# Second layer of a two-layer FFN kernel: x1's rows turned and gathered, output written by rows, stores issued by ScalarE

## Chip, cores and metric

The kernel runs on one core of one Trainium2 chip. The metric is the device time in microseconds (us) of one execution.

## The reference, cut to what matters

`x` has 32 samples of 128 channels by 2048 positions. Layer 0 ends in `x1`; the change is in layer 1 alone, and in how its inputs and outputs are moved.

```python
x = x + L0_ffn(L0_cond(x))                              # x1, the first layer
# layer 1, cond: nine taps, four groups of 32 channels, a bias of each sample and channel
z = conv_general_dilated(x1, weight, padding=[(4, 4)], feature_group_count=4)
z = z + ctx[:, :, None] + bias[None, :, None]
# layer 1, ffn: every row (sample, channel) of 2048 is permuted, cut into 16 heads of 128
t = z.reshape(b * l, Dm)[:, perm].reshape(b * l, h, d)
t = gelu(einsum('bhd,hdm->bhm', t, up), approximate=False)      # 128 -> 512
t = einsum('bhm,hmd->bhd', t, down).reshape(b * l, h * d)       # 512 -> 128
out = x1 + t[:, unperm]
```

## The kernel before, in words

Layer 1 works in 128 **units** and 128 **steps**. A unit `u` is the convolution of one sample and one group of 32 channels: four row blocks of 32 channels are loaded side by side into 128 partitions (`load_group`, L88, four loads), split by ScalarE (`xp_hi`, L1467) and VectorE (`xp_lo`, L1537) into a high and a low part, and multiplied on TensorE in nine products of 512 columns (L1426) into `ps_c`. ScalarE adds the bias and writes `z_s` (L1496), VectorE turns it in squares of 32 (L1559) into a tile in SBUF that has room for four units, and after each fourth unit (`u % 4 == 3`) the tile is stored to the DRAM scratch `z_d` by four stores, one for each 32 partitions (L1305, issued by SyncE). In `z_d` a row is a position, so that a permuted gather by rows does the `perm`.

A **block** is 16 units (four tiles) and then 16 steps, one for each head; there are 8 blocks. In step `s` GpSimd gathers 128 permuted rows of `z_d` into `t_s` (L1352, three steps ahead); ScalarE and VectorE split them (`t_hi` L1473, `t_lo` L1543); TensorE makes four `up` parts of three products (L1401) into `ps_up`; ScalarE takes the gelu of each into `kern` (L1479); the result is split into `g_hi` (a cast: parts 0 and 2 by ScalarE, L1483, parts 1 and 3 by VectorE, L1579) and `g_lo` (VectorE, L1581); TensorE makes four `down` parts of three products (L1411) into `ps_y`. ScalarE copies `ps_y` to `y_room` (L1516), and GpSimd scatters it to the rows of a second scratch, `y_d` (L1383), which does the `unperm`.

One block later SyncE loads rows of `y_d` back (L1269, pairs of steps), VectorE turns them (L1564) and adds x1 (L1570), which SyncE has loaded into `rear` (L1275), and SyncE stores the output (L1293). For the last block this would come at the end: there `y_d` is loaded into `w_hi`, TensorE transposes it (L1452), VectorE adds x1 (L1613) and SyncE and ScalarE store `out` (L1172).

All engines run the same sequence of steps, each with its own part: `LEAD` = 20, so step `s` has the convolution of unit `u = s + 20` beside it, and 20 units come ahead of step 0 (the **lead**). In a step TensorE makes the nine products of the convolution, then the parts `down(s, mc)` and `up(s+1, mc)` in turn. Each engine does its work in the order in which the program names it, its DMA issues too; a wait (`wait_ge`) for a semaphore holds all that stands behind it on that engine.

```python
            def store_z(k, h, parity):
                sp.wait_ge(zt_ready, u + 1)
                for r in range(2 if isinstance(u, int) and u == H - 1 else S):
                    sp.dma_start(z_rows(z_d[(parity + ahead) % 2], r, jb),
                                 zt_of(k, h)[r * GC:(r + 1) * GC].rearrange("p w b c -> p w (b c)")).then_inc(z_out[jb % 2], 16)
```

Of the kernel before, what the change touches and what calls it, by code (L numbers as in the profile page):

```python
# [28 lines left out]
Y_LO = 576  # L29
# [29 lines left out]
class Shared:  # L59
# [25 lines left out]
    def load_group(self, eng, x1_d, xp, j, b, g):  # L85

        for s in range(S):
            eng.dma_start(xp[s * GC:(s + 1) * GC, 1:Q + 1],  # L88
                          x1_d[b, g * GC:(g + 1) * GC, s, :]).then_inc(self.xp_in[j], 16)

# [55 lines left out]
def layer0_block(nc, block, sh, x, cond_w, bias_k, cond_t, w0, b0, w1, b1, w2, b2, w_t, bias, lora_a, lora_b, coeffs, scales,  # L146
                 conv_w, ctx_w, fside, ident, up, down, aggb_d, aggw_d, weff_d, t_d, u_d, x1_d):

    with ExitStack() as ctx:
# [43 lines left out]
        with ExitStack() as next_up:  # L193
            sh.ps_up = next_up.enter_context(nc.psum_tensor("ps_up", [P, MC, 512], F32))
# [860 lines left out]
def layer1_block(nc, block, sh, x1_d, up, down, perm, ident, z_d, y_d, out):  # L1055

    with ExitStack() as ctx:
# [16 lines left out]
        t_hi, t_lo = ([sb(f"{n}{j}", [P, RB], F32R) for j in range(2)] for n in ("t_hi", "t_lo"))  # L1074
        g_hi, g_lo = sb("g_hi", [P, MC, RB], F32R), sb("g_lo", [P, MC, RB], F32R)
        rear = sb("rear", [P, 4, 4 * P])
        yt_s, x1_s = (rear[:, 2 * j:2 * j + 2, :].rearrange("p a n -> p (a n)") for j in range(2))
        results = sb("results", [P, 2, 512])
        o_s = results[:].rearrange("p a n -> p (a n)")
        with ExitStack() as ahead:  # L1080
            second = ahead.enter_context(nc.sbuf_tensor("second_xp", [P, Y_LO + Q + 2], F32R))
        y_room = sb("y_room", [P, Y_LO + Q + 4])
        y_s = [y_room[:, j * Y_LO:j * Y_LO + RB] for j in range(2)]
        idx = sb("idx", [P, H], I32)
        id_s = sb("id_s", [P, P])
        xp, t_s, cbias = sh.xp + [o_s[:, 0:Q + 2]], sh.t_s, sh.cbias
        g_s = sh.kern[:].rearrange("p (c n) -> p c n", c=MC)

        zt_pair = [flat.rearrange("p (w b c) -> p w b c", w=WIDE, b=SB)
                   for flat in (sh.x1_s[:].rearrange("p a n -> p (a n)"), rear[:].rearrange("p w n -> p (w n)"))]  # L1090

        ps_up = sh.ps_up
        bank("up_room", MC)
        ps_c, ps_last = bank("ps_c"), bank("ps_last")
        ps_y = [bank(f"ps_y{j}") for j in range(2)]

        small_in, w_in = sem("small_in"), sh.w_in
# [3 lines left out]
        z_ready, zt_ready = sem("z_ready"), sem("zt_ready")  # L1101
        z_out = [sem(f"z_out{j}") for j in range(2)]
        t_in = [sem(f"t_in{j}") for j in range(2)]
# [59 lines left out]
        def last_unit(v):  # L1163

            return v % 4, v // 4
# [520 lines left out]
```

## Time and profile before

| | |
|---|---|
| median of 3 runs | 2507.52 us (2507.34 to 2511.15) |
| the profiled execution | 2513.49 us, its span 2511.7 us, mean clock of TensorE 0.989 |
| busy share of the span | TensorE 97%, VectorE 68%, ScalarE 44%, GpSimd 37% |
| first layer | up to about 1450 us |
| lead of the second layer | about 1460 to 1528 us |
| steps with a convolution | up to about 2346 us |
| steps without | up to 2479 us, then the last block's output up to 2512 us |

The profile is of one execution. Busy times are sums over an engine's instructions; the granted clock is a share of 2.4 GHz, so that 0.50 is 1.2 GHz. T is used for the moment at which a step's convolution begins. "SPq" and "ACTq" are the times for which the sequencers of SyncE and ScalarE are at DMA issues.

### The profile page before, as it was taken

The numbers are of one execution on the slowest core, as the hardware profiler recorded it, in microseconds if no ns is written. First come the engines' busy times: TensorE is split into PE (matmuls) and PEld (weight loads), VectorE is DVE, ScalarE is ACT, GpSimd is POOL, SyncE is SP. The second block draws the span as 40 slices with busy tenths as digits, with TensorE's granted clock in tenths as the row PEclk, the third lists the DMA queues.
The fourth block names the chain that finished last, engine by engine and source line by source line (L and its number), as shares of the span: only waits on it lengthen the run. The fifth ranks groups of instructions, "written<-read, shape, count | busy, mean of one in ns | idle before, by whom it ended". The sixth has DMA issues, their size and how long they took to land.

```text
span 2511.7 us, 37065 instructions
## 1 busy us (share of the span) xinstructions
PE 2432.4 (97%) x11130; PEld 2010.9 (80%) x11130; DVE 1713.9 (68%) x2449; ACT 1113.7 (44%) x1850; POOL 938.1 (37%) x826
## 2 busy tenths in 40 slices
PE   8899999999999999999999988999999999999985
PEld 6788888888888888887888866888888888888864
DVE  6665555875555855558544665778888888888865
ACT  3221211321212322223222356777777777777753
POOL 2275654556645255323233311222222222222331
PEclk9999999999999999999999999999999999999988
DMA  8965554755543767657555665468888888888898
GB/s 301 326 214 187 199 174 159 258 177 205 202 163 132 269 219 225 204 178 258 178 172 172 194 196 153 141 189 244 242 245 248 240 240 243 245 246 245 231 245 255
DMA packets 397563, 540.90 MB, mean 215 GB/s; under 512 B 37016, under 2 KB 262640, under 8 KB 397360
## 3 DMA queue, kind: packets, MB, share of 16 engines
q1 hardware_dynamic: 295872, 309.50, 43.0%
q10 hardware_dynamic: 77376, 152.17, 16.2%
q0 software_dynamic: 24112, 76.80, 9.9%
q8 instruction: 93, 1.52, 0.2%
q14 instruction: 110, 0.90, 0.1%
HBM read 309.72 MB, written 228.61 MB: 214 GB/s over the span
## 4 chain that ended last, share of the span: by engine, by line
PE 88%; DMA 5%; DVE 3%; issue 2%; SPq 1%; ACT 1%; POOL 0%; ACTq 0%; DVEq 0%; POOLq 0%
PE ps_c L463 45%; PE ps_up L1401 13%; PE ps_y L1411 13%; PE ps_c L1426 9%; PE ps_v L441 4%; PE ps_c L429 3%; DMA u_s<-z_d,idx 1%; DVE w_lo L1006 1%; PE ps_up L1426 1%; SPq L88 1%; DMA rear<-x_d 1%; DVE ring_lo L953 1%; DMA w_hi<-y_d 1%; DMA x_n<-in_up 0%; DVE x_s L1002 0%
## 5 line engine op out<-in xcount | busy, mean ns | idle before, releaser
L463 PE MATMUL ps_c<-w_hi,ring_hi 128*128 128x512 f32 x1792 | 703.9, 393 | 4.9 <-DVE r_early L1002 3.6
L463 PE MATMUL ps_c<-w_hi,ring_lo 128*128 128x512 f32 x1792 | 698.0, 390 | 0.0
L463 PE MATMUL ps_c<-w_lo,ring_hi 128*128 128x512 f32 x1792 | 697.9, 389 | 0.0
L613 ACT ACTIVATE ring_hi<-raw_n 128x512 fp32r<-128x512 f32 x382 | 239.6, 631 | 852.2 <-DVE raw_n L944 232.1
L1581 DVE TENSOR_TENSOR g_lo<-kern,g_hi 128x512 fp32r<-128x512 f32 x512 | 349.2, 687 | 80.3 <-ACT g_hi L1483 71.3
L463 PEld LDWEIGHTS ps_c<-w_hi,ring_hi 128*128 128x128 f32 x1792 | 336.8, 188 | 75.8 <-DVE ring_lo L953 4.7
L463 PEld LDWEIGHTS ps_c<-w_hi,ring_lo 128*128 128x128 f32 x1792 | 336.5, 188 | 69.8
L463 PEld LDWEIGHTS ps_c<-w_lo,ring_hi 128*128 128x128 f32 x1792 | 336.8, 188 | 67.5
L1383 POOL DMA_INDIRECT y_d<-y_room,idx x128 | 131.8, 1030 | 651.7 <-ACT y_room L1516 584.9
L1002 DVE TENSOR_TENSOR r_early<-ps_c,r_early 128x512 f32<-128x512 f32 x256 | 176.4, 689 | 275.9 <-PE ps_c L463 275.9
L1479 ACT ACTIVATE kern<-ps_up 128x512 f32<-128x512 f32 x512 | 304.5, 596 | 118.4 <-PE ps_up L1401 102.8
L953 DVE TENSOR_TENSOR ring_lo<-raw_n,ring_hi 128x512 fp32r<-128x512 f32 x382 | 327.6, 858 | 20.6 <-ACT ring_hi L613 20.2
L1002 DVE TENSOR_TENSOR x_s<-ps_c,x_s 128x512 f32<-128x512 f32 x192 | 132.4, 689 | 194.9 <-PE ps_c L463 194.7
L751 POOL TENSOR_TENSOR s<-raw_n 128x512 f32<-128x512 f32 x64 | 85.7, 1340 | 417.0 <-DMA raw_n<-u_d 311.4
L1411 PE MATMUL ps_y<-g_hi,w_hi 128*128 128x512 f32 x512 | 202.0, 394 | 12.8 <-DVE g_lo L1581 12.6
L1401 PE MATMUL ps_up<-t_hi,w_hi 128*128 128x512 f32 x512 | 201.8, 394 | 2.2 <-ACT z_s L1496 2.2
L1401 PE MATMUL ps_up<-t_lo,w_hi 128*128 128x512 f32 x512 | 201.3, 393 | 0.0
L1411 PE MATMUL ps_y<-g_lo,w_hi 128*128 128x512 f32 x512 | 201.2, 393 | 0.0
L1401 PE MATMUL ps_up<-t_hi,w_lo 128*128 128x512 f32 x512 | 200.8, 392 | 0.0
L1411 PE MATMUL ps_y<-g_hi,w_lo 128*128 128x512 f32 x512 | 200.3, 391 | 0.0
L1483 ACT ACTIVATE g_hi<-kern 128x512 fp32r<-128x512 f32 x256 | 162.5, 635 | 8.2
L1352 POOL DMA_INDIRECT u_s<-z_d,idx x128 | 129.9, 1015 | 87.4 <-DMA z_d<-rear 43.4
(188 smaller groups left out, 3628.0 us busy)
## 6 DMA issues: line engine op xcount, KB each, us to landing
u_d<-raw_n ACTq DMA_DIRECT2D x64, 512.0 KB, 3.2
x_d<-r_early ACTq DMA_DIRECT2D x128, 256.0 KB, 3.5
raw_n<-u_d SPq DMA_DIRECT2D x64, 512.0 KB, 3.6
x_d<-x_s ACTq DMA_DIRECT2D x126, 256.0 KB, 2.8
u_s<-x_d SPq DMA_DIRECT2D x496, 64.0 KB, 2.4
z_d<-x_s SPq DMA_DIRECT2D x120, 256.0 KB, 4.7
rear<-y_d SPq DMA_DIRECT2D x224, 128.0 KB, 3.7
rear<-x_d SPq DMA_DIRECT2D x56, 512.0 KB, 4.4
```

Of the source, the lines that this page charges most:

```text
L463: mm = nc.tensor.matmul(bank, a[:, dc, :], w[k][:, dc, :], start=(first and dc == 0 and n == 0), stop=(dc == 3 and n == 2), skip_group_che ...
L613: nc.scalar.activation(ring_hi[g % RING][:].rearrange("p a n -> p (a n)"), factor(q, k, p), ACT.Copy).then_inc(hi_ready, 1)
L953: nc.vector.tensor_tensor(ring_lo[g % RING][:].rearrange("p a n -> p (a n)"), factor(q, k, p), fp32(ring_hi[g % RING][:].rearrange("p a n ...
L1002: nc.vector.tensor_tensor(r_s[p][blk], bank, r_s[p][blk], ALU.add).then_inc((u_read if on_u else y_read)[p], 1)
L1352: nc.gpsimd.indirect_dma_start(out=t_s[j], out_offset=None, in_=z_d[parity], in_offset=bass.IndirectOffsetOnAxis(ap=idx[:, h:h + 1], axis= ...
L1383: nc.gpsimd.indirect_dma_start(out=y_d[parity], out_offset=bass.IndirectOffsetOnAxis(ap=idx[:, h:h + 1], axis=0), in_=y_s[j], in_offset=No ...
L1401: mm = nc.tensor.matmul(ps_up[:, mc, :], chunk(w, 2 * h)[:, mc * P:(mc + 1) * P], t, start=(n == 0), stop=(n == 2))
L1411: mm = nc.tensor.matmul(ps_y[h % 2][:, 0, :], chunk(w, 2 * h + 1)[:, mc * P:(mc + 1) * P], g[:, mc, :], start=(mc == 0 and w is w_hi and g ...
L1426: mm = nc.tensor.matmul(acc, w[:, 3 * g + tau, :], x[:, tau:tau + Q], start=(tau == 0 and n == 0), stop=(tau == 2 and n == 2))
L1479: nc.scalar.activation(g_s[:, mc, :], ps_up[:, mc, :], ACT.Gelu).then_inc(gelu_done, 1)
L1483: nc.scalar.activation(g_hi[:, mc, :], g_s[:, mc, :], ACT.Copy).then_inc(ghi_scalar, 1)
L1581: nc.vector.tensor_tensor(g_lo[:, mc, :], g_s[:, mc, :], fp32(g_hi[:, mc, :]), ALU.subtract).then_inc(glo_ready, 1)
```

## The change

Layer 0, the matrix products of layer 1 and their order stay. What changes:

- **x1 by rows.** The unit's x1, which is in SBUF for the convolution, is also turned by VectorE in squares of 32 (`turn_x`, L1433) into a tile of four units, and stored to a scratch `xt_d` like z to `z_d`. Units behind the lead with `u % 4 == 3` are turned one step ahead (`turned_early`), so that their tile is stored at the start of step `u`, ahead of z's.
- **Output by rows.** `out` has the rows of the permuted layout (the host's view of it is rearranged). GpSimd gathers 128 rows of `xt_d` into `rows` (L1227), VectorE adds `ps_y` to them (L1457) in place of ScalarE's copy, and GpSimd scatters the sum into `out` (L1234). `y_d`, the loads of it and of x1, y's turn, the additions of 1024 columns, the stores of SyncE and the whole last part (loads, transposes, 16 additions, 64 stores) go.
- **Who issues.** SyncE issues the unit loads only. All stores of z and of turned x1 are issued by ScalarE, four for each (`store_tile`, L1358).
- **Casts.** ScalarE makes those of parts 0, 2 and 3, VectorE that of part 1.
- **Buffers.** `ps_z0`, `ps_z1` are two banks for the convolutions throughout; xp's second pair lies over `t_hi` and `t_lo`; the first tiles lie in `rows`, `late_turned`; the unit loads wait also until x1 was turned; the load of unit 3 comes after the first layer's last product (`item_mm`), the wait for all first-layer row stores (`r_out`) at unit 4 instead of 0.
- **Loops** are written out: no Fori loops in layer 1.

```diff
         @block.sync
-            def load_rows(k, h, parity):
-            def load_final_x1(k, h):
-            def load_last_x1(c):
-            def finish():
-            def store_out(k, h):
-            def store_z(k, h, parity):
...
         @block.scalar
+            def store_tile(dram, tiles, stored, tile, quarters):
+                for r in quarters:
+                    act.dma_start(sh.turned_rows(dram[tile // G % 2], r, tile % G),
+                                 tile_of(tiles, tile)[r * GC:(r + 1) * GC].rearrange("p w b c -> p w (b c)")).then_inc(stored[tile % 2], 16)
+            def step(u, s):
+                if s >= 0 and s + 2 < STEPS:
+                    split_t(s + 2)
+                if u < STEPS and turned_early(u):
+                    store_x(u)
+                if s < 0:
+                    split_x(u + 1)
...
+                if u < STEPS:
+                    take_z(u)
+                if s >= 0 and u + 1 < STEPS:
+                    split_x(u + 1)
+                if u < STEPS and u % SB == SB - 1:
+                    store_z(u)
+                    if not turned_early(u):
+                        store_x(u)
+                if s < 0 <= s + 2:
+                    split_t(s + 2)
...
+                for mc in range(MC):
+                    if 0 <= s + 1 < STEPS:
+                        gelu(s + 1, mc)
         @block.vector
+            def turn_x(u):
+                tile = u // SB
+                if u % SB == 0:
+                    tile_free(dve, xt_out, tile)
+                nc.vector.transpose(tile_of(x_tiles, tile)[:, :, u % SB, :],
+                                    xp[xp_of(u)][:, 1:Q + 1].rearrange("p (w c) -> p w c", w=WIDE)).then_inc(xt_ready, 1)
+            def add_rows(s):
+                dve.wait_ge(down_done, MC * (s + 1))
+                dve.wait_ge(row_in[s % 2], 16 * (s // 2 + 1))
+                nc.vector.tensor_tensor(rows[:, s % 4, :], ps_y[s % 2][:, 0, :], rows[:, s % 4, :], ALU.add).then_inc(o_ready, 1)
         @block.gpsimd
+            def step(u, s):
...
+                if 0 <= s + AHEAD < STEPS:
+                    gather_t(s + AHEAD)
+                if 0 <= s + 2 < STEPS:
+                    gather_row(s + 2)
+                if s >= 0:
+                    scatter(s)
         @block.sync
+            sh.store_last()
+            sp.wait_ge(sh.item_mm, LAST)
+            load_rows(sp, 3)
```

ScalarE in one step behind the lead, before. `u_s` is the gathered tile or the unit's rows, `ps_c` the convolution, `kern` a gelu, `ps_y` the product of `down`:

```order
L1473 ACTIVATE t_hi<-u_s 128x512
L1496 ACTIVATE z_s<-ps_c,cbias 128x512
L1467 ACTIVATE xp_hi<-u_s 128x514
L1479 ACTIVATE kern<-ps_up 128x512
L1483 ACTIVATE g_hi<-kern 128x512
L1479 ACTIVATE kern<-ps_up 128x512 x2
L1483 ACTIVATE g_hi<-kern 128x512
L1516 ACTIVATE y_room<-ps_y 128x512
L1479 ACTIVATE kern<-ps_up 128x512
```

ScalarE in a step behind the lead that ends a tile, now. `x_turned` is the tile of turned x1, `x_s` lies where the tile of turned z does:

```order
L1345 ACTIVATE t_hi_room<-u_s 128x512
L1358 DMA xt_d<-x_turned 32x16x128 x4
L1337 ACTIVATE z_s<-ps_z,cbias 128x512
L1331 ACTIVATE xp_hi<-u_s 128x514
L1358 DMA z_d<-x_s 32x16x128 x4
L1350 ACTIVATE kern<-ps_up 128x512
L1354 ACTIVATE g_hi<-kern 128x512
L1350 ACTIVATE kern<-ps_up 128x512 x2
L1354 ACTIVATE g_hi<-kern 128x512
L1350 ACTIVATE kern<-ps_up 128x512
L1354 ACTIVATE g_hi<-kern 128x512
```

Four stores now stand between the split of t and z, four between the split of xp and the first gelu; y's copy is gone and the last gelu is followed by a cast. In the other three steps of a tile the two DMA rows are not there.

ScalarE at the end of the lead, before:

```order
L1473 ACTIVATE t_hi<-u_s 128x512
L1467 ACTIVATE xp_hi<-u_s 128x514
L1496 ACTIVATE z_s<-ps_up,cbias 128x512
L1473 ACTIVATE t_hi<-u_s 128x512
L1507 ACT_TABLE_LOAD
L1507 ACTIVATE y_room<-cbias 128x1
L1479 ACTIVATE kern<-ps_up 128x512
```

and the same place now:

```order
L1345 ACTIVATE t_hi_room<-u_s 128x512
L1331 ACTIVATE xp_hi<-u_s 128x514
L1337 ACTIVATE z_s<-ps_z,cbias 128x512
L1358 DMA z_d<-x_s 32x16x128 x4
L1358 DMA xt_d<-x_turned 32x16x128 x4
L1345 ACTIVATE t_hi_room<-u_s 128x512
L1350 ACT_TABLE_LOAD
L1350 ACTIVATE kern<-ps_up 128x512
```

All eight stores of the lead's last tile stand ahead of the second split of t and of the first gelu; so it is with the lead's other four tiles, whose eight stand behind z of their fourth unit.

VectorE behind the lead, now, in the step of a tile's third unit, in which the fourth unit's x1 is turned too, after its split:

```order
L1433 STREAM_TRANSPOSE x_turned<-u_s 128x16x32
L1439 TENSOR_TENSOR t_lo_room<-u_s,t_hi_room 128x512
L1426 STREAM_TRANSPOSE x_s<-z_s 128x16x32
L1415 TENSOR_TENSOR xp_lo<-u_s,xp_hi 128x514
L1433 STREAM_TRANSPOSE x_turned<-u_s 128x16x32
L1451 TENSOR_TENSOR g_lo<-kern,g_hi 128x512
L1447 CAST g_hi<-kern 128x512
L1451 TENSOR_TENSOR g_lo<-kern,g_hi 128x512 x2
L1457 TENSOR_TENSOR rows<-ps_y,rows 128x512
L1451 TENSOR_TENSOR g_lo<-kern,g_hi 128x512
```

The turns of x1 and the addition of `rows` are new in it; one of two casts is gone, and the work of 1024 columns that stood between `xp_lo` and the first `g_lo`.

## Rows read from the trace of the kernel before

**Rows 1.** Windows of layer 1: us, busy of PE, PEld, DVE, ACT, POOL; clock, DMA, GB/s

```profile
1460.00:1530.00 70.00, 51.45 (x182) 37.34 (x181) 33.19 (x52) 30.90 (x52) 6.30 (x10) 0.88 0.66 173
...
2020.00:2262.00 242.00, 242.00 (x1058) 198.56 (x1057) 205.40 (x319) 184.19 (x320) 64.64 (x64) 1.00 0.85 243
...
2346.00:2479.00 133.00, 119.97 (x496) 95.78 (x494) 105.36 (x163) 89.18 (x161) 41.36 (x39) 0.95 0.90 237
```

**Rows 2.** Timeline of TensorE: start, us, line, operation

```profile
1527.41 0.39 PE L1426 MATMUL ps_up<-second_xp,cw_lo 128*128 128x512 f32 x1
...
1536.54 0.39 PE L1411 MATMUL ps_y<-g_hi,w_hi 128*128 128x512 f32 x1
...
1783.92 0.39 PE L1426 MATMUL ps_c<-xp_hi,cw_hi 128*128 128x512 f32 x1
...
1786.02 0.39 PE L1411 MATMUL ps_y<-g_hi,w_hi 128*128 128x512 f32 x1
...
1793.58 0.39 PE L1411 MATMUL ps_y<-g_hi,w_hi 128*128 128x512 f32 x1
```

**Rows 3.** Timeline of ScalarE in the step from 1783.92

```profile
1784.96 0.63 ACT L1473 ACTIVATE t_hi<-u_s 128x512 fp32r<-128x512 f32 x1
...
1786.40 0.69 ACT L1496 ACTIVATE z_s<-ps_c,cbias 128x512 f32<-128x512 f32 x1 [0.81 <-PE ps_c L1426]
...
1787.60 0.60 ACT L1479 ACTIVATE kern<-ps_up 128x512 f32<-128x512 f32 x1
...
1788.23 0.63 ACT L1483 ACTIVATE g_hi<-kern 128x512 fp32r<-128x512 f32 x1
```

**Rows 4.** Timeline of VectorE in the same step

```profile
1787.12 0.71 DVE L1559 STREAM_TRANSPOSE x_s<-z_s 128x512 f32<-128x512 f32 x1 [0.17 <-ACT z_s L1496]
...
1791.62 0.69 DVE L1581 TENSOR_TENSOR g_lo<-kern,g_hi 128x512 fp32r<-128x512 f32 x1 [0.42 <-ACT g_hi L1483]
```

**Rows 5.** Timeline of SyncE's DMA queue: start, us held

```profile
1475.72 0.33 SPq L1305 DMA_DIRECT2D z_d<-x_s  x1
...
1477.67 1.44 SPq L1305 DMA_DIRECT2D z_d<-x_s  x1
...
1479.16 1.58 SPq L88 DMA_DIRECT2D u_s<-x_d  x1
...
2106.45 4.01 SPq L1305 DMA_DIRECT2D z_d<-x_s  x4
```

**Rows 6.** Timeline of the queues of ScalarE and SyncE

```profile
1519.02 0.51 ACTq L1501 DMA_DIRECT2D z_d<-rear  x1
...
1519.67 1.12 SPq L88 DMA_DIRECT2D u_s<-x_d  x1
...
2497.14 1.45 ACTq L1172 DMA_DIRECT2D out_dram<-u_s  x1
```

**Rows 7.** Timeline of TensorE, and windows behind two waits

```profile
2405.71 0.80 PE L1411 MATMUL ps_y<-g_hi,w_hi 128*128 128x512 f32 x1 [3.30 <-DVE g_lo L1581]
...
2404.50:2411.30 6.80, 5.59 (x13) 4.43 (x14) 6.37 (x10) 3.46 (x7) 2.18 (x2) 0.50 0.97 248
...
1530.70:1534.10 3.40, 3.40 (x10) 2.63 (x9) 1.25 (x3) 3.34 (x7) 1.53 (x2) 0.50 0.68 182
```

**Rows 8.** Groups by line: busy, mean ns; idle before, releaser

```profile
L1564 DVE STREAM_TRANSPOSE results<-rear 128x1024 f32<-128x1024 f32 x56 | 69.1, 1234 | 1.3 <-DMA rear<-y_d 1.3
...
L1579 DVE CAST g_hi<-kern 128x512 fp32r<-128x512 f32 x256 | 108.5, 424 | 26.2 <-ACT kern L1479 25.7
...
L1383 POOL DMA_INDIRECT y_d<-y_room,idx x128 | 131.8, 1030 | 651.7 <-ACT y_room L1516 584.9 <-issue 40.8 <-DMA rear<-y_d 26.0
```

**Rows 9.** Waits of TensorE (us, count, longest); timeline; DMA landing

```profile
PE ps_y L1411 <- DVE g_lo L1581: 12.6, 6, 4.4
...
2478.32 0.40 PE L1411 MATMUL ps_y<-g_hi,w_lo 128*128 128x512 f32 x1
...
y_d<-y_room,idx POOLq DMA_INDIRECT x128, 3.5
```

More of the change, by code:

```diff
@@ L1053, in _, with layer1_block @@
             take(LAST - 1)
-def layer1_block(nc, block, sh, x1_d, up, down, perm, ident, z_d, y_d, out):
+def layer1_block(nc, block, sh, x1_d, up, down, perm, z_d, xt_d, out):
     with ExitStack() as ctx:
@@ new lines, in load_rows, with turned_early, tile_of @@
+        def load_rows(eng, u):
+            _, b, g = place(u)
+            wait(eng, xlo_ready, last_xp_user(u) + 1)
+            wait(eng, xt_ready, last_xp_user(u) + 1)
+            if u == H:
+                for p in range(2):
+                    for blk in range(4):
+                        eng.wait_ge(sh.r_out[p][blk], 16 * QUADS)
+            sh.load_group(eng, x1_d, xp[xp_of(u)], xp_of(u), b, g)
+        def turned_early(u):
+            return u > LEAD and u % SB == SB - 1
+        def tile_of(tiles, tile):
+            return tiles[tile % 2 if tile < G else 1]
@@ new lines, in last_tile_user, with tile_free, block_stored @@
+        def last_tile_user(tile):
+            return tile - 2 if tile < G else tile - 1
+        def tile_free(eng, stored, tile):
+            last = last_tile_user(tile)
+            if last >= 0:
+                eng.wait_ge(stored[last % 2], 64 * (last // 2 + 1))
+        def block_stored(eng, stored, s):
+            if s % H == 0:
+                for j in range(2):
+                    eng.wait_ge(stored[j], 64 * 2 * (s // H + 1))
+        def by_scalar(mc):
+            return mc != 1
@@ L1392, in _, with up_part @@
+            drive(step)
+            for j in range(2):
+                pool.wait_ge(y_out[j], 16 * (STEPS // 2))
         @block.tensor
         def _(pe):
-            def up_part(k, h, mc):
-                s = H * k + h
+            def up_part(s, mc):
                 if mc == 0:
@@ new lines, in step @@
+            def step(u, s):
+                if s < 0:
+                    split_x(u + 1)
+                    for n in chunks_of(u):
+                        split_weights(n)
+                    turn_z(u)
+                    turn_x(u)
+                    if 0 <= s + 2:
+                        split_t(s + 2)
+                else:
+                    if u < STEPS and not turned_early(u):
+                        turn_x(u)
+                    if s + 2 < STEPS:
+                        split_t(s + 2)
+                    if u < STEPS:
+                        turn_z(u)
+                    if u + 1 < STEPS:
+                        split_x(u + 1)
+                        if turned_early(u + 1):
+                            turn_x(u + 1)
+                for mc in range(MC):
+                    if 0 <= s + 1 < STEPS:
+                        split_g(s + 1, mc)
+                    if s >= 0 and mc == MC - 2:
+                        add_rows(s)
```

533 lines of the change are left out of this document (170 added, 363 removed).

## The prediction

> **What bounds the kernel now.** I read the busy time by stage first, then one step of the second layer instruction by instruction. Three stretches of the second layer stand apart [rows 1]. In the 20 leading convolutions (1460 to 1530) TensorE is busy 51.45 of 70 us. In the steady stretch (2020 to 2262) it is busy throughout, with VectorE at 205.4 and ScalarE at 184.2 of 242 us. In the steps without a convolution (2346 to 2479) it is busy 119.97 of 133 us. Behind its last product the span has 33 us more. So the steady part can't get shorter, for the change leaves its matrix products as they are: it can win at the two ends and lose wherever another engine falls behind.
>
> How far behind may it fall? In a step whose convolution starts at T = 1783.92, the `down` products start at T+2.10, and those of the next step at T+9.66, so a step is 7.56 us [rows 2]. ScalarE splits the gathered tile at T+1.04, takes z at T+2.48, starts the first gelu at T+3.68 and the cast of it 0.63 later [rows 3]. The cast takes 0.63, VectorE follows ScalarE's end by 0.03 (as z's turn does z), and its subtraction takes 0.69 [rows 3, 4]. So `down` can start 0.63 + 0.63 + 0.03 + 0.69 = 1.98 us after the first gelu did, and that gelu may start at T+7.68 at the latest. Beyond that TensorE stands, as it does its work in order.
>
> **The stores on ScalarE's queue: the term that decides.** For each tile of four units the changed kernel issues four stores of z and four of turned x1, all with the 32x16x128 pattern that SyncE now issues. What does an issue cost the engine that makes it? On SyncE the first of four takes 0.33 us, the fourth 1.44, and the small load behind them is still held for 1.58; in the steady stretch four take 4.01 [rows 5]. So beyond the second each store waits for an earlier one to be worked off, one per about 1.45 us. Four cost 3.4 to 4.0. Eight in a row cost 0.4 + 6 x 1.45 plus a little, 9.3 us.
>
> Is ScalarE's queue spared? Its one pair of such stores takes up to 0.51, like the second on SyncE, and right after it SyncE's small load is held for 1.12 us; in the tail ScalarE's own issue is held for 1.45 us [rows 6]. I take it that ScalarE is held as SyncE is. The lower bound is 0.44 per issue (between the unheld 0.33 of [rows 5] and 0.51 of [rows 6]), the upper 9.3 for eight.
>
> The Trainium skill (DMA: Bandwidth & Descriptors, Issuing engines are not separate DMA queues) says that starting transfers on several engines saves only the sequencer's time for issuing, which is usually small. Taken as it stands this would make the eight issues cheap; [rows 5] show 3.4 us for four, and the sum by the rule is that of the first rival. The skill (Perfetto Trace Analysis, DMA Instruction — HWDGE) also says that such an instruction's window holds a wait for a shared generator and its work; [rows 6], where one queue's stores hold the other's load, agree.
>
> Now a steady step that ends a tile (u mod 4 = 3). y's copy on ScalarE goes and a cast (0.63) comes, so the step begins about where it did, with the split of t at about T+1.0 to 1.3. The four stores of x1 follow from T+1.4 and hold the engine for 3.4, to T+4.8. There z is taken, which could have been at T+2.48. z to its turned copy is 0.72 + 0.71 [rows 3, 4], so the stores of z begin at T+6.3. They come 4.9 us after the first store began, and the queue is not empty: by the pitch of [rows 5] the second of them is let go 6.4, the third 7.9 and the fourth 9.3 us after the first of the eight, T+10.75. The first gelu starts there, 3.1 us after the latest harmless moment. There are 27 such tiles (u = 23, 27, ... 127): 27 x 3.1 = 84 us. The slack outside the stalls lets ScalarE catch up before the next tile (1.8 us a step), so stalls don't pile up.
>
> A stall costs more than itself. After 3.30 us of waiting at 2405.71 the granted clock was 0.50 (1.2 GHz) until 2411.3, which cost half of 5.6 us; after the shorter wait before 1530 it was 0.50 for the 3.4 us from 1530.7 [rows 7], 1.7 us lost. For a stall of 3.1 I take 2.0, between 1.7 and 2.8 and nearer the lower since the step around it is denser: 27 x 2.0 = 54.
>
> **The leading units.** Here all eight stores stand in a row, after the last unit of a tile and before the split that the next but one convolution needs. A tile then takes: z 0.2 + 0.69 and its turn 0.72, eight issues 9.3, the two splits with their handovers 1.4, then three convolutions of 2.1 with a wait of about 1 us for x1's turn, which now releases the row buffer: about 19.7 us. Now 20 units take 67.8 us (1460 to the last product's end at 1527.8 [rows 2]), 13.5 a tile. Four intervals cost 4 x 6.2 = 25; the fifth tile's eight stores stand before the first gelu, and `down` starts 7 later than at 1536.54 counted from the last convolution [rows 2]. Sum +32, between +3 (unheld) and +40 (with clock falls). Two SyncE waits go here (z's stores no longer block the loads); the new holds are longer.
>
> **Other work, costed at nothing.** VectorE, a step: a cast of 0.42 goes, and half of y's turn of 1.23 and of the addition of like length [rows 8]; a turn of x1 (0.71) and an addition (0.69) come. That is 0.2 less, under TensorE. GpSimd issues three indirect transfers a step instead of two: 3 x 1.3 = 3.9 us (an estimate from their mean of 1.03 [rows 8] and the gap behind each) of 7.56, or of 5.44 without a convolution. Without that cover a late gather would hold ScalarE, as some do now. Total traffic falls from seven tiles of 256 KB a step to six. Loops are written out.
>
> **What is won.** Now TensorE waits 12.6 us for g_lo in six places [rows 9], nearly all of it after 2390, when gathers land late among the loads of x1 and y; with two falls of the clock (2.8 each) that is 18 us. Those loads go, a gather comes: I take 15, between 0 and 18. The tail: the last product ends at 2478.7 [rows 9] and the span at 2511.7. Afterwards an addition (0.69), the scatter's issue (1.03 [rows 8]), its landing (3.5 [rows 9]) and some 0.6 of handovers end near 2484.5: 27 us won, 26 to 28.
>
> **Sum.** 84 + 54 + 32 - 15 - 27 = +128 on a span of 2511.7. The profiled run took 2513.5 around that span, 6 above the median of the three runs, 2507.5; the difference is put on the median: 2635 us.
>
> **Rivals.**
> - *ScalarE's issues are cheap* (a fifth). 8 x 0.44 = 3.5 us of issues fit: x1's end at T+3.2, z's begin at T+4.6, the gelu comes at T+6.4, before T+7.68. Decision point: eight issues of 0.60 each (4.8 in all) still fit, longer ones don't. For it: ScalarE issues lone stores throughout the first layer unheld. Against it: [rows 5, 6]. Time: -27 - 15 + 3 = -39, 2468 us. This is the case on the other side. The Trainium skill (Perfetto Trace Analysis, DMA Optimizations) says that balancing transfers over the engines may help where generating them is the bottleneck; that rule speaks for it, and no trace here shows such a gain.
> - *Stalls without a clock fall* (0.14). For it: the shorter waits among those of [rows 9] left the clock at 1.00. Against it: [rows 7]. 84 + 32 - 42 = +74, 2581 us.
> - *The queue takes one store more before it holds* (0.14). The eight then end a pitch of 1.45 earlier: 1.65 us a tile remain, short enough to leave the clock, 45 us, and 25 for the lead: 45 + 25 - 42 = +28, 2535 us. With two more it would be about 0.2 a tile, and the whole turns to -19, 2488 us. For it: the four loads of y in the tail go out with little hold. Against it: [rows 5] in a quiet and in a busy stretch.
> - The change is in the program order (the order rows of ScalarE), so that it does nothing is out.
>
> **How the numbers follow.** Forecast 0.48, rivals 0.20, 0.14 and 0.14, rest 0.04. A change under 0.2% (5 us) is about what a measurement here can't tell from none. Slower: 0.48 + 0.14 + 0.08 + 0.01 = 0.71; same 0.04 (0.02 of the third rival, 0.02 of the rest); faster: 0.20 + 0.04 + 0.01 = 0.25. The forecast's own range is 2590 to 2680 (stalls of 2.4 to 3.7, clock 1.7 to 2.8, lead 20 to 40). To leave out no more than two in ten, the range is 2480 to 2680.
>
> **What would show it.** ScalarE's queue: store issues of 1 us and more, four taking 3.4 or more. TensorE waiting for g_lo once in four steps from 1570 on, about 27 times by 2 to 4 us, with falls of the clock behind it. Leading units spread over some 95 us. No idle gaps after the last convolution, and an end some 5 us after the last product. Wrong, if ScalarE's store issues are near 0.44.

## The result, and the profile after

The changed kernel takes 2671.28 us (median of 4 runs, 2669.17 to 2676.02) against 2508.05 us, a ratio of 1.0651 (95% interval 1.0632 to 1.0669). That is 163 us slower; the forecast was 128 slower, 2635 us, and the time lies within the range, 9 us under its upper end of 2680.

The page of the changed kernel, its span, engines, clock and chain:

```profile
span 2667.5 us, 34438 instructions
...
PE 2474.5 (93%) x11066; PEld 2033.4 (76%) x11066; DVE 1682.0 (63%) x2449; ACT 1127.3 (42%) x1849; POOL 1107.2 (42%) x961
...
PEclk9999999999999999999999788999999999999999
...
PE 72%; ACTq 9%; issue 5%; DVE 4%; DMA 3%; ACT 3%; POOL 2%; SPq 0%; DVEq 0%; POOLq 0%
```

The chain now has a share for ScalarE's queue, 9% at L1358, the stores; before it had none worth naming. The clock is granted at 0.7 to 0.8 in the slices of the lead. To see where the 163 us lie I cut both kernels at the same events: first convolution, first `down`, last convolution, last `down`, end. Windows of before, the first two (the third is in [rows 1]), and the last; columns as there:

```profile
1460.00:1537.00 77.00, 58.43 (x206) 42.92 (x205) 37.97 (x61) 37.01 (x63) 8.20 (x12) 0.87 0.67 176
1537.00:2346.00 809.00, 808.13 (x3528) 662.78 (x3527) 671.62 (x1053) 617.68 (x1070) 214.75 (x213) 1.00 0.80 226
...
2479.00:2512.00 33.00, 9.54 (x64) 8.62 (x64) 11.25 (x17) 0.35 (x1) 1.65 (x1) 0.72 0.82 286
```

and of the changed kernel:

```profile
1454.00:1571.00 117.00, 59.21 (x204) 43.51 (x202) 46.89 (x76) 32.87 (x56) 14.52 (x24) 0.79 0.63 167
1571.00:2541.00 970.00, 868.53 (x3530) 699.32 (x3531) 653.22 (x1076) 630.55 (x1075) 353.25 (x318) 0.93 0.62 172
2541.00:2661.00 120.00, 113.97 (x495) 93.24 (x493) 87.89 (x141) 93.23 (x160) 66.38 (x58) 0.97 0.48 143
2661.00:2668.00 7.00, 0.00 (x0) 0.00 (x0) 0.69 (x1) 0.00 (x0) 0.97 (x1) 0.79 0.20 75
```

The lead grew from 77 to 117 us, the steady part from 809 to 970; the steps without a convolution went from 133 to 120 and the end from 33 to 7. That sums to 40 + 161 - 13 - 26 = +162. (Layer 1 begins 5.8 us earlier in this profile. In the profiles of the experiments below it begins between 1453 and 1459 us, with layer 0 untouched, so that is scatter of one execution. It is also why the spans differ by 156 and the medians by 163.)

In the steady part TensorE's busy time itself grew from 808 to 869 us for the same products: 60 us of products at the lower clock. The other 101 us are idle. The waits of TensorE say what for:

```profile
PE ps_y L1289 <- DVE g_lo L1451: 117.1, 28, 9.9
PE ps_z L1303 <- issue: 35.2, 7, 9.5
PE ps_z L1303 <- DVE t_lo_room L1415: 12.8, 3, 9.7
```

Of the 28 waits for g_lo one is that of the first `down`, 9.9; the other 27, as many as there are tiles behind the lead, are 3.97 us in the mean: 26 in the steady part of 3.3 to 4.4 (mean 3.90), and the last tile's, 5.9, behind the last convolution. One of them in ScalarE's timeline and queue, in a step whose convolution starts at T = 2030.50:

```profile
2031.42 0.85 ACTq L1358 DMA_DIRECT2D xt_d<-x_turned  x2
...
2032.30 2.50 ACTq L1358 DMA_DIRECT2D xt_d<-x_turned  x2
2034.91 0.69 ACT L1337 ACTIVATE z_s<-ps_z,cbias 128x512 f32<-128x512 f32 x1 [2.42 <-issue]
...
2036.37 5.51 ACTq L1358 DMA_DIRECT2D z_d<-x_s  x4
2042.26 0.60 ACT L1350 ACTIVATE kern<-ps_up 128x512 f32<-128x512 f32 x1 [6.14 <-issue]
```

and TensorE's timeline at its end:

```profile
2044.36 0.79 PE L1289 MATMUL ps_y<-g_hi,w_hi 128*128 128x512 f32 x1 [4.05 <-DVE g_lo L1451]
```

The four stores of x1 hold the queue from T+0.9 to T+4.3, so z is taken at T+4.41. The four of z begin at T+5.87 and hold it for 5.51, and the first gelu starts at T+11.76, 4.08 after the T+7.68 that the prediction allowed. The product at 2044.36 waited 4.05 for it. Its duration is 0.79 in place of 0.39, and the products behind it are slower too. The window behind another such wait shows a granted clock of 0.50 (the last three numbers are clock, DMA share and GB/s):

```profile
1606.90:1613.70 6.80, 5.78 (x14) 4.52 (x15) 6.49 (x11) 5.87 (x12) 2.68 (x3) 0.50 0.32 89
```

The end is as the steps said. TensorE's last product in its timeline:

```profile
2660.59 0.40 PE L1289 MATMUL ps_y<-g_hi,w_lo 128*128 128x512 f32 x1
```

and VectorE's addition behind it, after which come only GpSimd's scatter (0.97 in the last of the windows above) and its landing, at 2667.5:

```profile
2661.02 0.69 DVE L1457 TENSOR_TENSOR rows<-ps_y,rows 128x512 f32<-128x512 f32 x1 [1.07 <-PE ps_y L1289]
```

### The profile page after: what moved, and what is told of

Read it like the earlier page. It is cut to its first block, busy times and chain, and to the rows that moved or that the text cites. A ratio compares the mean times of both kernels' runs of the same rounds, so it can differ in the third digit from the quotient of the medians.

```text
span 2667.5 us, 34438 instructions
## 1 busy us (share of the span) xinstructions
PE 2474.5 (93%) x11066; PEld 2033.4 (76%) x11066; DVE 1682.0 (63%) x2449; ACT 1127.3 (42%) x1849; POOL 1107.2 (42%) x961
## 4 chain that ended last, share of the span: by engine, by line
PE 72%; ACTq 9%; issue 5%; DVE 4%; DMA 3%; ACT 3%; POOL 2%; SPq 0%; DVEq 0%; POOLq 0%
PE ps_c L466 43%; PE ps_y L1289 10%; ACTq L1358 9%; PE ps_up L1280 9%; PE ps_z L1303 5%; PE ps_v L444 4%; PE ps_c L432 2%; ACT kern L1350 1%; DMA rows<-xt_d,idx 1%; POOL out_dram L1234 1%; DVE g_lo L1451 1%; DVE x_s L1426 1%; DVE w_lo L1009 1%; ACT z_s L1337 1%; ACT g_hi L1354 1%
## 5 line engine op out<-in xcount | busy, mean ns | idle before, releaser
L1234 POOL DMA_INDIRECT out_dram<-rows,idx x128 | 166.9, 1304 | 595.5 <-DVE rows L1457 595.5
L1289 PE MATMUL ps_y<-g_hi,w_hi 128*128 128x512 f32 x512 | 217.8, 425 | 117.2 <-DVE g_lo L1451 117.1
L1354 ACT ACTIVATE g_hi<-kern 128x512 fp32r<-128x512 f32 x384 | 243.3, 634 | 12.2
L1289 PEld LDWEIGHTS ps_y<-g_hi,w_hi 128*128 128x128 f32 x512 | 104.3, 204 | 152.4 <-DVE g_lo L1451 130.1
L1289 PE MATMUL ps_y<-g_lo,w_hi 128*128 128x512 f32 x512 | 210.7, 412 | 0.0
L1280 PE MATMUL ps_up<-t_hi_room,w_lo 128*128 128x512 f32 x512 | 209.1, 408 | 0.0
L1280 PE MATMUL ps_up<-t_hi_room,w_hi 128*128 128x512 f32 x512 | 209.1, 408 | 0.0
L1280 PE MATMUL ps_up<-t_lo_room,w_hi 128*128 128x512 f32 x512 | 209.0, 408 | 0.0
L1289 PE MATMUL ps_y<-g_hi,w_lo 128*128 128x512 f32 x512 | 208.7, 408 | 0.0
```

The source lines that it names most:

```text
L1234: nc.gpsimd.indirect_dma_start(out=out, out_offset=bass.IndirectOffsetOnAxis(ap=idx[:, s // H, h:h + 1], axis=0), in_=rows[:, s % 4, :], i ...
L1280: mm = nc.tensor.matmul(ps_up[:, mc, :], chunk(w, 2 * (s % H))[:, mc * P:(mc + 1) * P], t, start=(n == 0), stop=(n == 2))
L1289: mm = nc.tensor.matmul(ps_y[s % 2][:, 0, :], chunk(w, 2 * (s % H) + 1)[:, mc * P:(mc + 1) * P], g[:, mc, :], start=(mc == 0 and w is w_hi ...
L1354: nc.scalar.activation(g_hi[:, mc, :], g_s[:, mc, :], ACT.Copy).then_inc(ghi_scalar, 1)
```

## The experiments

Each diff below is an excerpt, in which ... stands for lines left out. Theory H, with which I went on, was the prediction's: ScalarE's store issues hold it, and nothing else costs. The table has each kernel's median with its ratio to the kernel before and, from its trace, the length of the lead (first convolution to first `down`), of the steady part (to the last convolution) and of the steps without a convolution. Before they are 76, 810 and 132, in the changed kernel 117, 970 and 120. e3, e4, e11 and e12 have two executions each, e7 three, the others four to ten.

| run | us | ratio (95%) | lead | steady | rest |
|---|---|---|---|---|---|
| e1 all stores by SyncE | 2533.7 | 1.0097 (1.0074 to 1.012) | 110 | 852 | 112 |
| e2 z's by SyncE | 2601.0 | 1.0379 (1.0355 to 1.0404) | 110 | 909 | 114 |
| e3 x1's by SyncE | 2586.7 | 1.0317 (1.0295 to 1.034) | 111 | 895 | 116 |
| e4 no early turn | 2725.6 | 1.0871 (1.0848 to 1.0894) | 119 | 1018 | 122 |
| e5 e1, z's first turn late | 2503.9 | 0.9997 (0.9987 to 1.0006) | 109 | 819 | 112 |
| e6 e5, x1's stores sooner | 2504.4 | 0.9991 (0.9981 to 1.0001) | 111 | 819 | 112 |
| e7 e1, x1's stores sooner | 2523.4 | 1.0063 (1.0042 to 1.0085) | 109 | 831 | 112 |
| e8 spread on ScalarE | 2506.0 | 1.0004 (0.9994 to 1.0013) | 118 | 811 | 112 |
| e9 e8, lead spread | 2486.9 | 0.9927 (0.9912 to 0.9942) | 94 | 814 | 112 |
| e10 before, z's by ScalarE | 2536.4 | 1.0121 (1.0103 to 1.014) | 83 | 824 | 135 |
| e11 sixteen halves | 2710.2 | 1.0815 (1.0792 to 1.0839) | 121 | 999 | 122 |
| e12 late turn only | 2673.5 | 1.0668 (1.0611 to 1.0726) | 117 | 967 | 121 |

**e1: all stores by SyncE.** `store_z` and `store_x` move to SyncE's step, behind its loads:

```diff
+        def z_by(u):
+            return "sp"
...
+        def x_by(u):
+            return "sp"
...
         @block.sync
...
+                if u < STEPS and u % SB == SB - 1:
+                    if x_by(u) == "sp" and turned_early(u):
+                        store_x(sp, u)
+                    if z_by(u) == "sp":
+                        store_z(sp, u)
+                    if x_by(u) == "sp" and not turned_early(u):
+                        store_x(sp, u)
```

> All z and x1 stores are issued by SyncE, behind its loads of the same step; nothing else differs from the changed kernel. Theory H (ScalarE is held by its store issues): no waits for g_lo of 1 us or more behind the first product of `down`, clock 1.00 there, so the 160 us that the steady part grew by go. In the lead SyncE has eight stores at 1.45 and sixteen loads at 0.45 a tile, about 17 to 19 us, a little under the present 21. Time 2490 to 2515. Rival B (the single tile buffers and late loads hold VectorE, whoever issues): waits of 1 us or more stay in most tiles, time 2550 or more. Rival C (the third cast makes ScalarE late): the waits stay at their size.

2534 us, 19 above the expectation. ScalarE's hold was the larger cost: 138 us went, and the waits for g_lo with it. The third cast is still ScalarE's here, so rival C falls. But TensorE now waits for xp_lo, which theory H did not have. Waits of TensorE (us in all, times, longest; 12.5 of them lie in the lead, so that 22 waits and 33.4 us are left behind it, 8.2 of these in the first step):

```profile
PE ps_z L1336 <- DVE xp_lo L1429: 45.9, 23, 12.5
```

waits of VectorE, the same columns (one, 6.0, in the lead):

```profile
DVE x_s L1440 <- DMA z_d<-x_s: 94.7, 27, 6.0
```

and the turn of z in VectorE's timeline:

```profile
2045.78 0.69 DVE L1453 TENSOR_TENSOR t_lo_room<-u_s,t_hi_room 128x512 fp32r<-128x512 f32 x1 [0.70 <-ACT t_hi_room L1378]
2050.78 0.71 DVE L1440 STREAM_TRANSPOSE x_s<-z_s 128x512 f32<-128x512 f32 x1 [4.31 <-DMA z_d<-x_s]
2051.42 0.65 DVE L1429 TENSOR_TENSOR xp_lo<-u_s,xp_hi 128x514 fp32r<-128x514 f32 x1
```

Behind the lead there is one tile buffer for z. The turn of the next tile's first unit waits until the last store of the tile before has landed, here 4.31 us, and xp_lo, which the next convolution needs, stands behind it on VectorE. In the changed kernel this wait does not appear: there the last store of z lands at T+14.6 (the middle one of 26 tiles), but ScalarE's hold delays that turn to T+17.6. In e1 the landing is at T+14.8 and VectorE is ready 3.4 us before it. The tile buffers are those of rival B, whose waits came (about half of the tiles by 1 us or more) and whose 2550 us did not. What I had not written down is that both could hold, one behind the other: one stall hid another.

**e2 and e3: one kind each.** As e1, for z's stores alone and for x1's alone; e2's edit is e1's with this difference; in e3 `z_by` returns "act" and `x_by` "sp".

```diff
+        def z_by(u):
+            return "sp"
...
+        def x_by(u):
+            return "act"
```

> Only the stores of z are issued by SyncE, those of x1 stay with ScalarE. Theory H: four issues hold ScalarE 3.4 us, z is taken at T+4.4 and the first gelu starts at about T+6, before T+7.68: no wait in the steady part. Lead about 17 us a tile. Time 2485 to 2510. Rival B: waits stay, 2550 or more.

2601 us: missed by 91. The waits for g_lo went, as the slack said (three are left), but VectorE waits for z's stores 28 times, 110.6 us in all, and TensorE for xp_lo 27 times, 65.3 us, with falls of the clock behind the longer ones.

> Only the stores of x1 are issued by SyncE, those of z stay with ScalarE. Theory H: z's stores begin at T+3.9 on an empty queue and hold 3.5 to 4, so the first gelu starts at T+7.5 to T+8.1: waits of 0 to 0.5 us a tile, no falls of the clock. Time 2495 to 2525. If z's stores hold 5.4 as they do in the changed kernel (because of what GpSimd and SyncE have under way, not of x1's stores ahead of them), waits of 1.5 us and 2535 to 2560.

2587 us: missed by 62. The branch named last in the expectation comes nearest, but its 2560 is passed as well; the waits for g_lo behind the first `down` are 2.0 us in the mean. ScalarE issues only z's four stores here, and they hold it for as long as in the changed kernel, while x1's four come from another queue. The reason may be these four, or what GpSimd and SyncE have under way besides; e4 and e7 below tell them apart. ScalarE's queue and timeline:

```profile
2035.57 6.00 ACTq L1189 DMA_DIRECT2D z_d<-x_s  x4
2041.67 0.60 ACT L1383 ACTIVATE kern<-ps_up 128x512 f32<-128x512 f32 x1 [6.35 <-issue]
```

So what holds an issue is not the issuer's own queue alone. Over the 26 or 27 tiles z's four take 5.4 us (0.36 + 1.81 + 1.81 + 1.42) in the changed kernel with x1's on the same queue, 5.7 with them on SyncE's, but 3.8 in e10, where no store is under way before them. The Trainium skill (DMA: Bandwidth & Descriptors, Issuing engines are not separate DMA queues) says that transfers run on the same 16 DMA engines whichever engine started them, and that issuing from several saves only sequencer time, "which is usually small relative to the DMA itself". Of the first e3 is in line. Of the second the runs show the exception: the sequencer time of one engine was worth 138 us to e1.

**e4: x1's stores behind z's.** `turned_early` returns False, so all eight stores stand between xp's split and the first gelu.

```diff
         def turned_early(u):
-            return u > LEAD and u % SB == SB - 1
+            return False
```

> x1 of a tile's fourth unit is turned in its own step, and the four stores of x1 stand behind those of z. Theory H: the eight issues begin at T+3.9 in place of T+0.9, and with about 9 us of them the first gelu starts at T+13: waits of 5 to 5.5 us in place of 4.0, 27 times, and longer falls of the clock. Time 2700 to 2740. Rival: if the queue were held by what x1's stores leave in it and not by the number of issues, the time stays within 10 us of 2671.

2726 us, as expected. Eight in a row in ScalarE's queue and timeline, and the gelu behind them:

```profile
2022.24 3.79 ACTq L1358 DMA_DIRECT2D z_d<-x_s  x4
2026.15 5.39 ACTq L1358 DMA_DIRECT2D xt_d<-x_turned  x4
2031.64 0.60 ACT L1350 ACTIVATE kern<-ps_up 128x512 f32<-128x512 f32 x1 [10.06 <-issue]
```

3.79 + 5.39 = 9.2 us, the 9.3 of the prediction for eight. The early turn is worth 54 us. The waits grew from 3.9 to 5.8 us each, a little more than expected, but the falls of the clock did not: TensorE is busy for 867 us of the steady part, as in the changed kernel (869).

**e5, e6, e7: the tile buffer.** e5 is e1 with VectorE's order changed: the turn of z of a tile's first unit comes behind the step's g_lo. e6 and e7 are e5 and e1 with x1's stores one step sooner.

```diff
         @block.vector
-                    if u < STEPS:
+                    if u < STEPS and u % SB:
                         turn_z(u)
...
                 for mc in range(MC):
                     if 0 <= s + 1 < STEPS:
                         split_g(s + 1, mc)
...
+                if s >= 0 and u < STEPS and u % SB == 0:
+                    turn_z(u)
```

and for e6 and e7:

```diff
         @block.sync
+                if u + 1 < STEPS and turned_early(u + 1):
+                    store_x(sp, u + 1)
                 if u < STEPS and u % SB == SB - 1:
-                    if x_by(u) == "sp" and turned_early(u):
-                        store_x(sp, u)
                     if z_by(u) == "sp":
                         store_z(sp, u)
```

> e1 (all stores by SyncE), and VectorE turns z of a tile's first unit behind the g_lo of its step, not ahead of xp_lo. In e1 that turn waited 4.3 us for the last store of the tile before, and the next convolution waited for xp_lo behind it. If the single tile buffer is what binds e1, its turn may now come some 4 us later at no cost: the steady part (first `down` to last convolution) falls from 852 to 810 to 820, time 2492 to 2503. Rival (late loads of x1 or late gathers behind the stores bind e1): it stays at 845 or more, time 2525 or more.

2504 us, 1 above the expectation; the steady part fell from 852 to 819 us, the waits of VectorE for z_d behind the lead are gone, and with them the second cost. This is the time of the kernel before, neither better nor worse.

> e5, and SyncE issues x1's four stores one step sooner, as soon as the early turn is done. Buffer theory: nothing is left to win over e5 or up to 8 us, steady part 810 to 813, time 2488 to 2500. If SyncE's loads, which then stand behind a wait for the turn, become late: new waits for xp_lo behind DMA u_s, time over 2510.

2504 us, 4 above the expectation, with 819 us in the steady part where 810 to 813 were expected: e6 wins nothing over e5. Of the 819 some 8 us are one wait in the first step, where VectorE waits 9.2 us for the stores of the lead's last tile of x1.

> e1 with x1's stores one step sooner, z's first turn where it was. z's stores then land 1 to 2 us sooner, of the mean wait of 1.6 us in e1 0 to 0.7 is left: steady part 812 to 830, time 2495 to 2515. If the pitch of the stores is set by what else is under way and not by x1's stores ahead of them, it stays within 5 us of e1.

2523 us, 8 above the expectation, though TensorE's waits for xp_lo behind the lead fell from 33.4 us in 22 to 16.0 in 12. VectorE still waits for z_d 27 times (83.2 us). SyncE's queue in one tile of e1 and in one of e7 says why:

```profile
2038.13 7.65 SPq L1189 DMA_DIRECT2D z_d<-x_s  x4
...
2027.28 3.18 SPq L88 DMA_DIRECT2D u_s<-x_d  x4
2030.50 4.11 SPq L1189 DMA_DIRECT2D z_d<-x_s  x4
```

Over the tiles behind the lead z's four take 6.2 us in e1 (1.35 + 1.74 + 1.69 + 1.42) and 3.9 in e7 (0.41 + 0.51 + 1.16 + 1.79), which is what they take in e10 and in the kernel before (3.8, 3.7). In e4, where x1's four come behind z's, it is 3.7 too. GpSimd's three transfers a step are there in both. So the longer hold of z's four, in e3 also, comes from x1's four just before them. It did not become time, because four loads now stand between x1's stores and z's and are themselves held (3.18 for four), so that z's first store begins at T+5.6 in place of T+3.8 and its last lands only 1.0 us sooner (T+13.8 for T+14.8).

**e8: apart, on ScalarE.** All eight stores stay with ScalarE: x1's four behind the four gelus of the step before, two of z's at their place, two behind the first gelus; z's first turn late.

```diff
         @block.scalar
...
-                store_tile(z_d, z_tiles, z_out, tile, range(S))
+                store_tile(z_d, z_tiles, z_out, tile, range(2 if u >= LEAD else S))
...
-                if u < STEPS and turned_early(u):
-                    store_x(u)
...
                 for mc in range(MC):
                     if 0 <= s + 1 < STEPS:
                         gelu(s + 1, mc)
+                    if s >= 0 and u < STEPS and u % SB == SB - 1 and mc < 2:
+                        quarter(u, 2 + mc, z_d, z_tiles, z_out)
+                    if u + 1 < STEPS and turned_early(u + 1):
...
+                        quarter(u + 1, mc, xt_d, x_tiles, xt_out)
```

> All eight stores stay with ScalarE behind the lead, but apart: x1's four one each behind the gelus of the step before, z's first two at their place, the other two behind the first two gelus; z's first turn late as in e5. The lead is that of the changed kernel. Theory H in its form of the prediction (an issue holds the engine only while earlier stores are being worked off): the issues take 0.3 to 0.6 each, no wait of 1 us or more for g_lo, steady part 810 to 825, time 2510 to 2530. Rival (eight issues cost ScalarE their 9 us wherever they stand): waits for g_lo of 2 us or more stay, 2580 or more.

2506 us, 4 better than the lower bound. The queue of ScalarE in one tile:

```profile
2019.76 0.36 ACTq L1358 DMA_DIRECT2D xt_d<-x_turned  x1
...
2021.49 0.31 ACTq L1358 DMA_DIRECT2D xt_d<-x_turned  x1
...
2022.86 1.01 ACTq L1358 DMA_DIRECT2D xt_d<-x_turned  x1
...
2025.98 2.08 ACTq L1358 DMA_DIRECT2D z_d<-x_s  x2
...
2028.80 0.84 ACTq L1358 DMA_DIRECT2D z_d<-x_s  x1
```

and the windows of the lead and of the steady part:

```profile
1458.30:1575.90 117.60, 60.92 (x203) 44.62 (x201) 46.50 (x76) 33.54 (x57) 14.66 (x24) 0.76 0.62 165
1575.90:2387.40 811.50, 811.50 (x3531) 664.65 (x3532) 651.84 (x1075) 624.49 (x1075) 368.44 (x319) 1.00 0.71 206
```

The issues take 0.3 to 1.3 each in the mean over the tiles, the longest 2.3, not the 0.3 to 0.6 that was expected: x1's four 2.2 in sum, z's 4.0, 6.2 for the eight in place of 8.8. The steady part is 811.5 us with TensorE busy throughout, at clock 1.00: the same number of issues, by the same engine, costs TensorE nothing where they are apart. Two things changed at once, which the run does not part: the issues are shorter, and only two of them (1.6 us) still stand between xp's split and the first gelu. Either is theory H's. This is the sharpest of the runs for it, and what it leaves is the lead, 118 us.

**e12: the control of e8.** Besides the stores e8 also changed z's first turn; this is that late turn alone (the diff of e5, on the changed kernel).

> The changed kernel with e8's late turn of z alone; ScalarE issues as before, eight stores close together. In the changed kernel VectorE nowhere waits for a stored z tile, for ScalarE's hold comes first. If spreading the issues is what e8 won by, this changes nothing: 2660 to 2675, waits for g_lo of 4 us, 27 times. If the late turn was what counted, the time falls to 2600 or less.

2673 us, no change: the late turn by itself is worth nothing, and e8 did not win by it alone. Stores spread without the late turn were not run.

**e9: the lead too.** Tiles 0 to 2: one store of z by SyncE and one of x1 by ScalarE in each of the next four units; tile 3 at once, one kind each; tile 4 by SyncE, off the first gelu's path. Both turns of unit 20 stand behind its step's g_lo.

```diff
+        def lead_stores(eng, u, store):
+            if SB <= u < H:
+                store(eng, SB * (u // SB) - 1, (u % SB,))
+            if u == H - 1:
+                store(eng, u)
...
         @block.sync
...
+                lead_stores(sp, u, store_z)
+                if u == LEAD - 1:
+                    store_z(sp, u)
+                    store_x(sp, u)
...
         @block.scalar
...
+                lead_stores(act, u, store_x)
```

> e8, and the lead's stores apart too: of tiles 0 to 2 one store of z by SyncE and one of x1 by ScalarE in each of the next four units; tile 3 at once, z by SyncE and x1 by ScalarE; tile 4's eight by SyncE, so that the first gelu doesn't stand behind them; both turns of unit 20 behind its step's g_lo. Theory: the lead's 117 us are 76 plus eight issues in a row at five places. Three places go, two shrink: lead 85 to 98, the steady part 810 to 822, time 2475 to 2492, and so faster than the kernel before for the first time. Rival (the lead is bound by buffers, loads or VectorE's new turns, not by the row of eight): lead 108 or more, time 2500 or more.

2487 us, within the expectation, and the only kernel that beats the one before (0.9927, interval 0.9912 to 0.9942), by 19 us. Its windows:

```profile
1458.00:1552.00 94.00, 60.51 (x205) 43.78 (x204) 47.00 (x77) 34.36 (x59) 14.63 (x24) 0.85 0.72 184
1552.00:2366.00 814.00, 810.70 (x3532) 664.47 (x3531) 649.90 (x1074) 623.50 (x1074) 372.94 (x320) 1.00 0.71 208
2366.00:2479.00 113.00, 112.54 (x494) 92.16 (x492) 87.22 (x142) 93.07 (x160) 67.40 (x58) 1.00 0.49 147
```

The lead is 94 us, still 17 above that of before, with waits of 6.9 and 5.1 us around unit 15, where tile 3's stores still stand together because tile 4 takes the same buffer: ScalarE's four issues of x1 take 6.3 there, and VectorE waits 6.9 for z's four to land.

**e10: one part of the change alone.** The kernel before with z's four stores issued by ScalarE behind xp's split, in the lead too; x1's path is as it was.

```diff
         @block.sync
-                if exists(k, h, LEAD) and (h + LEAD) % G == G - 1:
-                    store_z(k, h, parity)
...
         @block.scalar
...
                     if not lead(k) and exists(k, h, LEAD + 1):
                         split_x(*after(k, h))
+                if exists(k, h, LEAD) and (h + LEAD) % G == G - 1:
+                    store_z(act, k, h, parity)
```

> The kernel before with one part of the change alone: z's four stores are issued by ScalarE behind xp's split, the rest is as it was. By the slack (first gelu at T+7.68 at the latest) and the hold of four (3.4 to 4.0, begun at T+3.9) the gelu comes at T+7.4 to T+8: waits of 0 to 0.3 us, the steady part 810 to 820; the lead 5 to 15 us longer, since ScalarE's splits stand behind four issues. Time 2508 to 2530. If ScalarE is held as long as in e3 (6.0): waits of 2 us and 2570 or more.

2536 us, 6 above the expectation. ScalarE's queue in one tile, and the gelu behind:

```profile
2025.73 3.80 ACTq L1249 DMA_DIRECT2D z_d<-x_s  x4
2029.71 0.60 ACT L1477 ACTIVATE kern<-ps_up 128x512 f32<-128x512 f32 x1 [4.23 <-PE ps_up L1399]
```

and the waits of TensorE for g_lo:

```profile
PE ps_y L1409 <- DVE g_lo L1577: 25.0, 21, 4.1
```

Four issues alone take 3.80 and just exceed the slack: many short waits, the steady part 824 in place of 810, the lead 83 in place of 76. Moving z's stores to ScalarE by itself costs 31 us. (Most of the 25.0 us lie in the first `down` and behind the last convolution, where the kernel before has its 12.6 [rows 9].)

**e11: what the hold is a price of.** Each of the eight stores is cut into two with half of the rows.

```diff
                 for r in quarters:
+                    for w in (slice(0, WIDE // 2), slice(WIDE // 2, WIDE)):
-                    act.dma_start(sh.turned_rows(dram[tile // G % 2], r, tile % G),
+                        act.dma_start(sh.turned_rows(dram[tile // G % 2], r, tile % G)[:, w, :],
...
```

> The changed kernel with each of the eight stores cut into two of half the rows. If a store holds the engine until an earlier one's bytes are worked off, sixteen halves hold it about as long as eight wholes (8.8 us), a little less as more fit in unheld or a little more for 16 fixed parts: waits of 3.5 to 5 us, time 2650 to 2700. If the hold is a price of each issue (about 1.45 whatever its size), sixteen take 20 us or more: waits of 12 us, time 3000 or more.

2710 us, 10 above the upper end of the first branch and far from the second. Two rows of ScalarE's queue:

```profile
2052.47 0.82 ACTq L1359 DMA_DIRECT2D xt_d<-x_turned  x2
...
2053.32 4.92 ACTq L1359 DMA_DIRECT2D xt_d<-x_turned  x6
```

The eight halves of x1 take 5.7 us and those of z 4.3 (means over the tiles), 10.0 for sixteen against 8.8 for eight. So a store has no fixed price of 1.45; what it holds goes with its size. That the two sums lie near each other is in part chance: an issue that nothing holds takes 0.31 alone and 0.5 behind another, sixteen of them 7.6, so that the halves are held for only some 2.4 us beyond that and the eight whole ones (3.6 unheld) for 5.2. With x1's halves holding longer, z and xp are taken later, and TensorE waits for xp_lo as well (34.3 us in 26), which the expectation left out.

## Why the prediction was right

**The bound and the slack held.** The steady part is TensorE's and could only get longer; T+7.68 as the last harmless moment gives waits of 4.08 from a gelu at T+11.76, where 4.05 was measured, and in e10 the gelu behind 3.80 us of issues starts at T+7.9 in the middle one of the tiles, with waits of 0.1 to 1.2 us, the edge of it.

**ScalarE is held as SyncE is.** The rival of cheap issues (0.20) fell: the first issue takes 0.31, those behind it 0.7 to 1.8 in the mean. The rival in which the queue takes one store more fell too. The place, the count (27) and the engine waited for came out as said.

**The stall's size: 3.1 forecast, 3.97 measured.** The terms: x1's issues began at T+0.9 (T+1.4 forecast) and took 3.4 (3.4), z's began at T+5.87 (T+6.3); z's four then took 5.5 where 4.45 were put, and 0.4 lay between their end and the gelu, which I left out. The step that was mis-sized is "by the pitch of [rows 5]": a pitch of 1.45 was read from four stores with none before them, and the second four meet x1's, which are still landing (7.7 us from issue to landing for the last of them in this tile). The eight end 10.5 us after the first began, where 9.3 were forecast; in e4, eight on end, 9.2 came out. With x1's four out of the way z's take 3.9 (e7). This made the 84 us about 101 (idle in the steady part).

**The clock: 54 forecast, 60 measured** as additional busy time of TensorE (869 - 808), or 2.2 us for each of 27 waits (26 and that of the first `down`) where 2.0 was taken. The rival without it (0.14) fell.

**The lead: +32 forecast, +40 measured,** the upper end named. The clock falls there too, which the +32 left to the upper bound: behind a hold the first convolution takes 3.97 us (1503.77 to 1507.74) in place of the 2.1 of the forecast, 1.9 a tile. ScalarE's queue and timeline in the lead:

```profile
1475.30 5.11 ACTq L1358 DMA_DIRECT2D xt_d<-late_turned  x4
1480.51 0.63 ACT L1331 ACTIVATE t_hi_room<-u_s 128x514 fp32r<-128x514 f32 x1 [9.45 <-issue]
```

x1's four take 5.11 behind z's four, and the split behind them has waited 9.45 for the eight.

**What was won: 15 and 27 forecast, 13 and 26 measured.** In the steps without a convolution one tile's wait is left, 5.9 us (2541 to 2661 has it); without it they take 112 (e8), which is the work of TensorE. So the nearness of 13 to 15 is luck: 21 us were won there, more than the 18 named as the most, and 8 lost again to a stall and the clock behind it.

All three costs were put too low (84 + 54 + 32 against 101 + 60 + 40), by 31 us together, and the gains 3 us too high; the range held them because it had room for more, not because its terms were exact.

**What the forecast lacked** did not show in its number: that the single tile buffers would bind next. e1 and e2 had to show it. With stores off ScalarE the changed kernel is still 1.0 to 3.8% slower than before. In e1, the 1.0%, the lead has 34 us more than before and the steady part 42, against 20 and 26 won behind them; most of the 42 is a wait that the steps never costed. The forecast was right on the kernel as written, but a reader who drew from it that moving the stores back to SyncE mends the change would have been 20 to 90 us off, as I was.

What stays open: what sets the pitch of 1.4 to 1.9 us a store. e11 says that it falls with the amount, e3 that the two queues share it, and e7 that it needs other stores just before; whether packets or bytes set it was not parted.

## What to carry to other kernels

A DMA issue cost its engine little here with none under way (0.3 to 0.5 us), and 1 to 2 us behind other stores. So put the issues of a burst apart, between other work of the issuing engine, before moving them to another queue, and count them on the engine whose lateness the critical engine sees.

When a stall is found, ask what would be late next without it, and read that from the order and the buffers: here a wait for a single tile buffer stood right behind the hold, and with the stores on SyncE only both mends together (e5) gave the time back; neither the move alone (e1) nor the late turn alone (e12) did. (e8 has both too, but its stores were not spread without the late turn.)

Count a wait of TensorE with the clock that follows it: 4 us cost half as much again here.

## What was not expected of the hardware

Two queues don't divide the hold: z's four stores held ScalarE 5.7 us with x1's issued by SyncE, 5.4 with all on one queue, 3.8 with none beside them; on SyncE's queue they held it 6.2 us right behind x1's (e1) and 3.9 with x1's a step sooner (e7); on ScalarE's, with x1's behind them, 3.7 (e4).

The price in clock differs with the wait. Against the 811.5 us that TensorE is busy in e8's steady part, it is busy 57 us more in the changed kernel (26 waits, 3.9 us in the mean), 56 in e4 (5.8), 32 in e3 (895 us, of them 843.87 busy; 26 waits, 2.0 in the mean), and 7.5 in e1, whose waits behind the first step are 2.5 us and less. So the price rises with the wait up to some 2.2 us and no further between waits of 3.9 and 5.8:

```profile
1564.30:2416.70 852.40, 819.02 (x3532) 664.74 (x3531) 652.52 (x1074) 644.92 (x1074) 353.56 (x320) 0.99 0.70 199
```
